# Weight scales in pairs at the end of a step, a Newton step on GpSimd, and a second staging buffer in a gated feed-forward kernel

## The reference, cut to what matters

```python
scale = cond @ norm_w.T + 1.0                              # (8, 512)
ms = mean(x * x, -1)                                       # x: (8, 512, 512) f32
h = x * (scale[:, None, :] * rsqrt(ms + EPS))
u = h @ up_w.T                                             # up_w: (4096, 512)
val, gate = split(u, 2, -1)
h = val * gelu(gate, approximate=False)                    # (8, 512, 2048)
hq = act_quant(h)                                          # 127 levels by row maximum
wq = weight_quant(down_w)                                  # ternary, one scale; down_w: (512, 2048)
y = hq @ wq.T + x
```

## Time and profile before

| | us |
|---|---|
| runs of the kernel before | 785.71, 789.64, 789.03 (median 789.03) |
| profiled execution | 786.19 |
| its span, first to last instruction | 784.4 |
| PE busy in the span | 758.4 (97%) |
| DVE, ACT, POOL busy | 611.4, 428.3, 264.4 |
| granted TensorE clock, mean | 0.987 |

### The profile page before, as it was taken

How to read it: one execution, slowest core, us unless ns; L and a number is a source line. 1 busy time by engine, 2 the same in 40 slices (tenths; PEclk the granted TensorE clock), 3 DMA queues, 4 the chain that set the end, 5 groups by cost and what they waited for, 6 DMA issues and landing times.

```text
span 784.4 us, 17750 instructions
## 1 busy us (share of the span) xinstructions
PE 758.4 (97%) x6306; PEld 623.3 (79%) x6306; DVE 611.4 (78%) x852; ACT 428.3 (55%) x1002; POOL 264.4 (34%) x318
## 2 busy tenths in 40 slices
PE   5899998999899999999999999999999999999998
PEld 3688887888688877888788877888788877888653
DVE  5989997799867985788767985788767985775667
ACT  5688777677556543654346543654346543454233
POOL 4677975546412321224112421223112421111111
PEclk9799999999899999999999999999999999999999
DMA  6476777776695668656686658655685658465332
GB/s 207 168 262 221 252 247 236 274 268 207 175 322 196 215 182 242 240 204 169 193 304 200 214 174 246 235 210 161 199 301 200 215 172 246 172 213 179 105 132 83
DMA packets 82255, 165.50 MB, mean 211 GB/s; under 512 B 47100, under 2 KB 47652, under 8 KB 82212
## 3 DMA queue, kind: packets, MB, share of 16 engines
q1 hardware_dynamic: 81668, 164.66, 64.1%
q10 hardware_dynamic: 544, 0.27, 0.1%
HBM read 131.73 MB, written 22.17 MB: 196 GB/s over the span
## 4 chain that ended last, share of the span: by engine, by line
PE 77%; DVE 3%; DMA 2%; issue 0%; ACT 0%; SPq 0%; DVEq 0%; ACTq 0%
PE A L1209 12%; PE A L1212 12%; PE A L1211 12%; PE Y L1259 11%; PE B L1212 9%; PE B L1209 9%; PE B L1211 9%; DVE h L984 1%; DMA xT<-xf 1%; DMA wslots<-w_scratch 1%; PE X L1248 1%; DVE q L998 0%; PE S L1254 0%; PE A L1259 0%; DVE q L1007 0%
## 5 line engine op out<-in xcount | busy, mean ns | idle before, releaser
L1209 PE MATMUL A<-xT,wslots 128*128 (+1 forms) x1024 | 280.5, 274 | 7.3 <-ACT snapC L692 5.6
L1211 PE MATMUL A<-xT,wslots 128*128 (+1 forms) x1024 | 280.3, 274 | 0.0
L1212 PE MATMUL A<-xT,wslots 128*128 (+1 forms) x1024 | 280.3, 274 | 0.0
L556 POOL TENSOR_TENSOR snapC<-snapC 128x256 f32<-128x256 f32 x128 | 107.7, 841 | 447.0 <-ACT snapC L692 444.4
L1209 PE MATMUL B<-xT,wslots 128*128 (+1 forms) x768 | 210.7, 274 | 0.0
L1212 PE MATMUL B<-xT,wslots 128*128 (+1 forms) x768 | 210.7, 274 | 0.0
L1211 PE MATMUL B<-xT,wslots 128*128 (+1 forms) x768 | 210.7, 274 | 0.0
L950 DVE SCALAR_TENSOR_TENSOR h<-h,c_all,g 128x512 f32<-128x512 f32 (+1 forms) x128 | 102.8, 803 | 99.6 <-ACT g L715 99.1
L1209 PEld LDWEIGHTS A<-xT,wslots 128*128 128x128 f16 x1024 | 100.5, 98 | 24.5 <-ACT snapC L692 7.6
L1211 PEld LDWEIGHTS A<-xT,wslots 128*128 128x128 f16 x1024 | 100.6, 98 | 14.4
L1212 PEld LDWEIGHTS A<-xT,wslots 128*128 128x128 f16 x1024 | 100.7, 98 | 12.1
(11 more groups left out here) (149 smaller groups left out, 907.6 us busy)
## 6 DMA issues: line engine op xcount, KB each, us to landing
wslots<-w_scratch SPq DMA_DIRECT2D x105, 896.0 KB, 4.7
w_scratch<-wslots SPq DMA_DIRECT2D x15, 896.0 KB, 4.6
wst<-in_L_cond_up_w_dram SPq DMA_DIRECT2D x16, 512.0 KB, 6.0
xin<-in_x_dram SPq DMA_DIRECT2D x8, 1024.0 KB, 7.3
dwb<-in_L_cond_down_w_dram SPq DMA_DIRECT2D x16, 512.0 KB, 4.8
wst<-in_x_dram SPq DMA_DIRECT2D x28, 256.0 KB, 5.6
out_dram<-wst SPq DMA_DIRECT2D x28, 256.0 KB, 5.2
scl_b<-scl_rows SPq DMA_DIRECT2D x6, 256.0 KB, 7.5
```

What stands on the lines that cost most here:

```text
L556: pool.tensor_tensor(snapC[:, s % 2, 0:H], snapC[:, s % 2, 0:H], snapC[:, s % 2, H:T], ALU.add)\
L1209: pe.matmul(into, high, xh, start=(start and kp == 0), stop=False, skip_group_check=not start)
L1211: pe.matmul(into, high, xl, start=False, stop=False, skip_group_check=not start)
L1212: mm = pe.matmul(into, low, xh, start=False, stop=last, skip_group_check=not start)
```

## The change

Three edits.

1. `w_scale` is taken apart. `w_largest(s+4)` stands at the end of DVE's step s, between `w_low(s+1, 2)` and `largest(s-1)`, in place of `w_scale(s+3)` near the start. `w_inverse` is made for two tiles at once after every second one (list `SCALED`). For tiles 0 to 2 the order stays; `w_largest(3)` is done ahead of the loop.
2. `rms(1)` and `refine(1)`, five DVE instructions on 128x4 values, become `root(1)` on POOL in step 3, with the power between them.
3. In batch 1 (x of batch 2) half kp = 1 is staged in `wst` slots 0 and 1 (`xstage2`). ACT no longer waits for the transposing DMA of kp = 0 there. SP waits for the DMA of kp = 1 before it loads the first `xres`.

```diff
+    SCALED = [(0, 1), (1, 1), (2, 1), (3, 2), (5, 2), (7, 2), (9, 2), (11, 2), (13, 2), (15, 1)]
+    INVERSE_AT = {p + n - 4: i for i, (p, n) in enumerate(SCALED) if i > 2}
...
+        def xstage_of(b, kp):
+            return xstage2 if isinstance(b, int) and b == 2 and kp else xstage1
...
                 else:
+                    sp.wait_ge(x_turned_in[KP - 1], 16 * (b - 1))
                     load_xres(b - 2, 0)
...
+            def root(b):
+                pool.wait_ge(squares_ready, b + 1)
+                pool.tensor_scalar(ms[:, :], ss[:, :], 1.0 / D, RMS_EPS, ALU.mult, ALU.add).then_inc(ms_ready, 1)
+                rsqrt(b)
+                pool.wait_ge(pow_ready, b + 1)
+                pool.tensor_tensor(r_a[:, :], r_pow[:, :], r_pow[:, :], ALU.mult).then_inc(newton_steps, 1)
...
+                pool.tensor_tensor(rstd[:, :], r_pow[:, :], r_a[:, :], ALU.mult).then_inc(rstd_ready, 1)
...
-                if s == RMS_AT_0:
-                    rsqrt(1)
+                if s == ROOT_AT_0:
+                    root(1)
...
-                    if kp:
+                    if kp and isinstance(b, int) and b == 2:
+                        act.wait_ge(mix_steps, MIX * FT)
+                    elif kp:
                         act.wait_ge(x_turned_in[0], 16 * (b - 1))
...
+            def w_inverse(i):
+                p, n = SCALED[i]
+                some = slice(VG * p, VG * (p + n))
+                dve.wait_ge(w_max_ready, p + n)
...
             c_first(0, 3)
             w_low(0, 3)
+            w_largest(3)
 
             for s in range(FT):
                 if s > 0:
                     value(0, s - 1)
-                if s + 3 < FT:
-                    w_scale(s + 3)
-                if s == RMS_AT_0:
-                    rms(1)
-                if s == REFINE_AT_0:
-                    refine(1)
...
                     hidden(0, s - 1)
                 if s + 1 < FT:
                     w_low(s + 1, 2)
+                if s + 4 < FT:
+                    w_largest(s + 4)
+                    if s + 1 in INVERSE_AT:
+                        w_inverse(INVERSE_AT[s + 1])
                 if s > 0:
                     largest(0, s - 1)
                 if s + 1 < FT:
                     w_low(s + 1, 3)
```

More of the change, by code:

```diff
@@ L182, in gated_ffn_program @@
         squared = xf1[:, 0:TT * D // 2].bitcast(F16).rearrange("p (t d) -> p t d", d=D)
-        xstage = xf1[:, :].bitcast(F16).rearrange("p (a n) -> p a n", a=2)
+        xstage1 = xf1[:, :].bitcast(F16).rearrange("p (a n) -> p a n", a=2)
+        xstage2 = wst[:, 0:2, :, :].rearrange("p w v d -> p (w v d)")[:, 0:NB * H].bitcast(F16)\
+            .rearrange("p (a n) -> p a n", a=2)
         q32 = q[:, :].bitcast(F32)
@@ L665, in x_high_stage @@
             def x_high_stage(b, kp, cut):
+                stage = xstage_of(b, kp)
                 act.wait_ge(xmix_steps, 8 * b + (4 * kp + (4 if cut else 2)))
                 if cut == 0:
[L668 removed]
+                    if kp and isinstance(b, int) and b == 2:
+                        act.wait_ge(mix_steps, MIX * FT)
+                    elif kp:
                         act.wait_ge(x_turned_in[0], 16 * (b - 1))
[L670 removed]
+                    act.activation(stage[:, 0, 0:4 * H].rearrange("p (h t n) -> p h t n", h=2, n=P), xn_blocks(kp),
                                    ACT.Copy).then_inc(xhi_ready, 1)
                 else:
[L673 removed]
+                    act.activation(stage[:, 0, 4 * H:NB * H], xsum[:, :], ACT.Copy).then_inc(xhi_ready, 1)
             def w_high(p, c):
@@ L889, in x_low_stage @@
             def x_low_stage(b, kp, cut, nth):
+                stage = xstage_of(b, kp)
                 dve.wait_ge(xhi_ready, 4 * b + nth)
                 if cut == 0:
-                    high, low = [xstage[:, i, 0:4 * H].rearrange("p (h t n) -> p h t n", h=2, n=P) for i in range(2)]
+                    high, low = [stage[:, i, 0:4 * H].rearrange("p (h t n) -> p h t n", h=2, n=P) for i in range(2)]
                     dve.tensor_tensor(low, xn_blocks(kp), high, ALU.subtract).then_inc(xlo_ready, 1)
@@ L895, in x_low_stage @@
                 else:
-                    dve.tensor_tensor(xstage[:, 1, 4 * H:NB * H], xsum[:, :], xstage[:, 0, 4 * H:NB * H], ALU.subtract)\
+                    dve.tensor_tensor(stage[:, 1, 4 * H:NB * H], xsum[:, :], stage[:, 0, 4 * H:NB * H], ALU.subtract)\
                        .then_inc(xlo_ready, 1)
-            def w_scale(p):
-                w_largest(p)
-                w_inverse(p)
             def w_largest(p):
-                pair = slice(VG * p, VG * p + VG)
                 dve.wait_ge(w_loaded[p % WSTAGE], 16 * (p // WSTAGE + 1))
-                dve.tensor_reduce(inv_w[:, pair], wst[:, p % WSTAGE, :, :], AX.X, ALU.max,
-                                  apply_absolute_value=True).then_inc(w_steps, 1)
@@ L909, in w_inverse @@
[L909 to L915, removed]
+                dve.tensor_reduce(inv_w[:, VG * p:VG * p + VG], wst[:, p % WSTAGE, :, :], AX.X, ALU.max,
+                                  apply_absolute_value=True).then_inc(w_max_ready, 1)
@@ L916, in w_inverse @@
+            def w_inverse(i):
+                p, n = SCALED[i]
+                some = slice(VG * p, VG * (p + n))
+                dve.wait_ge(w_max_ready, p + n)
+                dve.tensor_scalar(c_w[:, some], inv_w[:, some], TINY, 1.0 / W_GAIN, ALU.max, ALU.mult).then_inc(w_steps, 1)
+                dve.wait_ge(w_steps, 2 * i + 1)
+                dve.tensor_scalar(c_w[:, some].bitcast(I32), c_w[:, some].bitcast(I32), EXPONENT, None,
                                   ALU.bitwise_and).then_inc(w_steps, 1)
-                dve.wait_ge(w_steps, 3 * p + 3)
@@ L918, in w_inverse @@
-                dve.reciprocal(inv_w[:, pair], c_w[:, pair]).then_inc(w_scale_ready, 1)
+                dve.wait_ge(w_steps, 2 * i + 2)
+                dve.reciprocal(inv_w[:, some], c_w[:, some]).then_inc(w_scale_ready, n)
             def w_low(p, c):
@@ L1072, in _ @@
             dve.tensor_reduce(brow[:, :], BA[1][0:B, 0:P], AX.X, ALU.max).then_inc(scl_steps, 1)
-            w_scale(0)
+            w_largest(0)
+            w_inverse(0)
             dve.wait_ge(bmax_psum, 1)
@@ L1095, in _ @@
             w_low(0, 2)
-            w_scale(2)
+            w_largest(2)
+            w_inverse(2)
             c_first(0, 3)
             w_low(0, 3)
+            w_largest(3)
             for s in range(FT):
```

10 lines of the change are left out of this document (8 added, 2 removed).

## The result

The changed kernel takes 804.78 us (median of 4 runs, 804.01 to 805.2) where the kernel before, in the same comparison, takes 788.29: 1.0221 times as long, 95% interval 1.0197 to 1.0244. Its profiled execution took 804.01 us, 17.82 more than the profiled one of before (786.19), with a span of 802.4.

A forecast was written before the change was run, and what follows sets the result against it. PE, busy 97% of the span, was taken as the bound. 786.19 + 18.4 - 3.1 = 801.5 us from the profiled execution, 804.3 from the median; the middle, 803, was forecast, range 796 to 814.

The forecast's parts named there:

- The ring: Batch 0: w_low(s, 3), store, load, w_largest(s+4), w_low(s+1, 3) close a loop within one step; +18.4 us.
- G: Batch 0: time from the end of w_low(s, 3) to a possible w_largest(s+4), taken as 6.2 us.
- The signs named for the profile: Batch 0: w_largest waits 2 to 4 us in nearly each step; PE's w_low waits reach 15 us or more.
- The Newton step: Edit 2, batch 0: DVE's saving only becomes waiting for the DMA, and POOL's added instructions are covered; 0 us.
- faster: Rival: loads land before DVE asks, so waits in batch 0 and 3.1 us of batch 1 are won; 782 us, chance 0.06.
- The second staging buffer: Edit 3, batch 1: ACT's wait and the low-clock stretch go, PE gains 3.1 us; bounds 2.4 and 5.2.
- moves up by that much and no more: Batch 1: the chain behind x_low_stage, with the second turn_x and slot loads, comes 2.37 us earlier.
- The wait for slot 1: Step 1 of batch 2: the slot load, landing 0.7 us before PE began, would limit PE's gain to 2.4 + 0.7 us.
- no change: Rival: G falls to 5.15 us, batch 0 loses 6.8, batch 1 wins 3.1; 791 us, chance 0.06.
- Slower still, by the clock: Rival: PE's gaps in batch 0 lower the clock each turn, 9.3 us more; 812 us, chance 0.12.
- a fall or two: Batch 0: this many drops of the clock would be swallowed by PE's idle time.

The follow-up runs named there:

- pairs_only: The kernel before with edit 1 alone (largest values at the end of the step ahead, paired inverses): 804.49 us, ratio 1.0236.
- newton_only: The kernel before with edit 2 alone (mean square and Newton step of the second x on POOL): 783.99 us, ratio 0.9968.
- stage_only: The kernel before with edit 3 alone (second half of batch 1's x staged in the weight slots): 786.17 us, ratio 0.9997.
- load_first: The changed kernel with SP issuing the load ahead of the store, still after the slot's low parts are done: 789.68 us, ratio 1.0041.
- merge_behind: The changed kernel with the merges of the row maxima (largest(s-1)) moved behind w_low(s+1, 3): 797.08 us, ratio 1.0118.
- stage_xlow_early: The kernel before with edit 3, and DVE's low staging of x's second half ahead of q's scale and rounding in batch 1: 782.28 us, ratio 0.9948.
- best: The changed kernel with each load ahead of the store, for the slot freed a step ago, early low staging, slot 14 and last packed load before the first turn: 779.25 us.
- best_no_pairs: The kernel before with edits 2 and 3, early low staging, and slot 14 and the last packed load ahead of the first turn: 779.64 us, ratio 0.9896.

## Why the prediction was right, and where it was not

**The ring (+18.4 forecast, +17.68 measured, 18.2 counted from step 1): right, and nearly so term by term.** The first turn was to start at 35.6 us; `w_low(1, 3)` ends at 35.47. G was put at 6.2; it is 6.38 and 6.91 in the first two turns and 5.95 to 6.06 in the other nine, 6.12 in the mean. (In the first two a load of down_w is near, issued at 33.31 and 47.21 us; but beside the one issued at 62.13 G is 6.05, so that this is the reason isn't shown.) Turns without the inverse are 7.5 us, the first 7.9 (7.77 forecast), turns with it 8.2 to 8.8 (8.35), those with a merge 10.3, 12.6 and 10.2 (9.6, 13.2 and 10.5). The eleven turns take 97.1 us (97.7), so `w_low(12, 3)` ends at 132.6 (133.3). What made this possible is that all durations in the loop were in the rows before, and only the order was new. The signs named for the profile came, too: eleven waits on the DMA of `wst`, 3.0 us each in the mean, and PE's waits on `w_low` up from 1.9 to 13.8 us, a little under the 15 named. The range was not added up rightly at its low end: G at 5.99 and all of batch 1 give 786.19 + 16.1 - 5.2 = 797.1, not 796. The long steps 6 and 9 are DVE's; on ACT's mark they are steps 7 and 10 (13.4 and 11.4 us), which need what DVE makes there.

**The Newton step (0 forecast): right inside the ring, under its own condition.** The prediction said that what edit 2 saves only turns into DVE's wait for the DMA; pairs_only and after bear that out to 0.03 us. `w_mix(5)` did wait for the paired inverse, 1.25 us more behind POOL's five instructions, so these cost nothing there. Its price outside the ring was mis-sized: rival "faster" gave it some 0.8 us, newton_only 1.6 in step 4 and 2.3 of the time. The bound of up to 5 us for POOL's instructions was far too wide; they take 1.0 us together.

**The second staging buffer (-3.1 forecast, +0.1 measured): wrong.** The step that failed is "moves up by that much and no more": I let the second `turn_x` move up by the whole 2.37 us that DVE had waited for ACT, and then looked for what is late next among the slot loads alone. In after ACT's wait is gone as forecast and no clock falls behind it; measured from step 28, DVE begins the low staging 2.44 us earlier, and step 31 comes after 16.61 us instead of 20.69. So 4.1 us were won there. Then PE met the turned x. The chain of waits in 224 to 240 us (start, us, what) shows it:

```profile
224.61 1.14 DVE h L1008
...
225.78 1.50 DVE q L1013
...
229.40 0.88 DVE wst L924
230.27 0.02 issue
230.29 7.85 DMA xT<-wst
238.14 0.40 issue
238.54 0.28 PE A L1234
```

The low staging's second half (L924) stands behind the scale and rounding of q. Those took 1.49 us at L1013 and 0.83 at L1018, while POOL worked on `dwb` and `snapC` beside them; in the kernel before the same two took 0.69 and 0.43, and POOL had ended its work on `dwb` 0.27 us ahead of them. The rounding and what POOL did beside it, in after and then in before, where POOL did nothing:

```profile
225.69 1.04 POOL L615 TENSOR_SCALAR dwb<-dwb 128x1024 f32<-128x1024 f32 x1
225.78 1.49 DVE L1013 TENSOR_SCALAR q<-h 128x1024 f16<-128x1024 f32 x1
```

```profile
210.52 0.69 DVE L989 TENSOR_SCALAR q<-h 128x1024 f16<-128x1024 f32 x1
```

That is 1.2 of the 2.44 us, and the second turn went out only 1.25 us earlier. In stage_only it is 1.0 us, at the merge of the row maxima (1.25 us instead of 0.69) and at the same rounding (1.09), and the turn goes out 14.90 us behind step 28, about as late. (That POOL is the cause is read from the traces; no run took POOL's work away.) Then the turn took 7.85 us to land where it had taken 6.10. From step 28, x was there at 16.39 + 6.10 = 22.49 us before and at 15.14 + 7.85 = 22.99 after: half a microsecond later, for a PE that came 4 us earlier. PE waited 2.4 us for it, and from 238.9 us on the clock was at the lower level (1.2 GHz) for 3.4 us, which at half speed costs about 1.7: 4.1 together, all that had been won. Its price can be checked: load_first and merge_behind have this wait of PE, too (2.4 and 2.8 us), without a fall behind it, and take 28.70 and 28.85 us from step 28 to step 33 where after takes 30.53. The windows before and in that fall (us, PE, PEld, DVE, ACT, POOL busy, granted clock, DMA share, GB/s):

```profile
232.00:239.00 7.00, 4.56 (x46) 3.82 (x44) 6.17 (x8) 3.08 (x7) 1.43 (x2) 0.99 1.09 270
238.90:242.30 3.40, 3.40 (x19) 2.43 (x18) 0.00 (x0) 0.77 (x2) 0.00 (x0) 0.50 1.01 426
```

stage_xlow_early, best and best_no_pairs bear this account out: in the first the turn is issued 11.7 us behind step 28 instead of 15.1 and takes 6.09 us, so it lands before PE asks, the clock stays up, and the gain is 4.5 us, inside the 2.4 to 5.2 that I had put as bounds. The prediction had also said that PE itself waits for that DMA before p1 of batch 2. I used it to cost SP's new wait at nothing and did not ask when the DMA lands. The wait for slot 1, which I had put last in line, did not come; PE waited 1.1 us for slot 14 instead.

**The rivals.** "Faster" needed G under 4.3 us and "no change" 5.15; it was 6.1. load_first reached 4.6 by another order of SP's queue. "Slower still, by the clock" did not come: of the eleven turns only three were followed by a fall, from 54.6, 88.7 and 116.0 us on, and those are the three with a merge in them, in which PE's wait was longest. Two of the falls and the stretch between them, in windows of after (columns as above):

```profile
54.60:58.00 3.40, 3.40 (x19) 2.47 (x17) 1.66 (x3) 2.41 (x6) 3.32 (x5) 0.50 0.99 313
58.00:88.70 30.70, 24.46 (x214) 21.26 (x212) 19.09 (x28) 20.30 (x47) 18.26 (x27) 1.00 0.55 188
88.70:95.50 6.80, 5.83 (x28) 4.71 (x29) 3.44 (x7) 2.60 (x6) 3.32 (x5) 0.50 0.65 212
```

PE has time for them: at full clock it is busy for 24.5 of 30.7 us. The ring's end at 132.6 us is the one that DVE's chain alone gives, and so the falls cost nothing, as the forecast had it for "a fall or two"; pairs_only has two of the three falls, from 88.2 and 115.5 us on, and the same 122.03 us. The Trainium skill, "TensorE: Matmul & The Clock Gate", section "HAM oscillation — how this bites in real kernels", has the clock fall in every turn of a loop in which TensorE's work in a turn is shorter than the wait for a DMA. Here the work is the longer of the two (24.5 us busy of 30.7), so the prediction read that rule more widely than it stands; the clock fell in 3 turns of 11, and the 812 us did not come.

**The sum.** 801.5 against the profiled execution became 804.01, and 804.3 against the median became 804.78: 0.7 too much in batch 0, 3.2 too little in batch 1. The median shown before, 789.03, came from three runs; the kernel before had 786.3 to 787.4 in the later comparisons, so the profiled execution was the better base, and the higher one hid part of the miss in batch 1. That 803 came within 2 us of 804.78 is in part luck: a little too much in the ring, too little in batch 1 and a base that was too high offset one another.

## What to carry to other kernels

Before an instruction that waits is moved to a later place in its queue, follow what is queued behind it: if one of these releases the very load that it waits for, the loop closes, and its turn (here 6.1 + 1.6 us and the merges, where rows of the kernel before had given 6.2 + 1.6) takes the place of the step. Such a loop is opened at either end, by the order of the waiting engine or by that of the queue that loads, and it is harmless while its turn is shorter than the step. And when a stall is removed, trace every input of the instruction that will be next in line with its own landing time: a gain in one chain is cut off by the slowest of the others, as the turned x did to a buffer that was worth 4.5 us once DVE's queue was reordered as well.

## What the runs showed of the hardware

**A packet of the instruction queue beside the transposing DMA.** In batch 1 each kernel issues two turns. Of these 28 turns in fourteen profiled executions, the 23 that have a packet of 16384 bytes of the instruction queue about 5.8 to 6.0 us behind their issue land after 7.8 to 8.3 us, and the five that have none after 6.1. The table of queues and issues in 230 to 238 us of after and in 213 to 220 us of before (queue, packets, MB, share; then KB each and us to landing):

```profile
q8 instruction: 1, 0.02, 0.7%
...
xT<-wst SPq DMA_TRANSPOSE x1, 7.8
```

```profile
q1 hardware_dynamic: 3630, 1.02, 80.5%
...
xT<-xf SPq DMA_TRANSPOSE x1, 6.1
```

It isn't the source tile: pairs_only turns from `xf` and has 7.93. Whether that packet holds the transfer up, or both are held by a third thing, was not tried.

**DVE beside POOL.** The rounding of q at L1013 took 1.49 us when it began behind an instruction of POOL that was still running (225.69, above), and 0.69 without. With the tiny instructions it is the same: from 20 us on, the first of `w_inverse` (L937) took 0.17 us in each of the six places in after where POOL ran nothing beside it, as at 84.33 above, where POOL itself was waiting for the inverse, and 0.53 and 0.33 in the two where POOL did. Its counterpart in the kernel before (L912) began while an instruction of POOL was running in eleven of fourteen places. It took 0.44 to 0.75 us in six of these, 0.23 and 0.24 in two and 0.17 in three: what counts is how much of POOL's instruction is left. In the eight longer ones DVE's instruction ends 0.02 to 0.03 us behind POOL's, and in the three of 0.17 no more than 0.14 us was left. One of them, with POOL's:

```profile
106.63 0.73 POOL L545 TENSOR_TENSOR q<-q 128x256 f32<-128x256 f32 x1
```

```profile
106.75 0.64 DVE L912 TENSOR_SCALAR c_w<-inv_w 128x2 f32<-128x2 f32 x1
```

The first of `refine` took 0.54 beside POOL and 0.15 to 0.16 in the six later batches. Where DVE was first it was not held: the rounding at 231.43 us in after took 0.69, and the instruction that POOL began 0.14 us behind it took 1.13 where most of its kind take 0.73. Nor does all of POOL's work hold DVE: beside its power (L529) the rounding at 243.57 us in before took 0.69. The Trainium skill, "SBUF — State Buffer", section "Who interferes with whom", says that DVE's two-input instructions, and in some modes its tensor-scalar ones, contend with GpSimd for a shared port, and that in those modes the one that issues first keeps it for its whole instruction; the trace agrees in the rows above, but for that exception.

**The clock and the length of a wait.** In after, a wait of PE of 2.5 us, the longest on `S` above, was followed by the lower clock from 54.6 us on. In merge_behind one of 3.0 us was not, nor was there any fall in that kernel from 34 us until its last microsecond (its waits of PE in 20 to 160 us):

```profile
...
PE B L1234 <- DVE h L968: 3.9, 2, 3.0
...
```

The length of the wait alone doesn't decide it; what else does was not tried.
